# Multi-head graph attention on one core: scores' row left in PSUM, layer 3's score stage ahead of the values' linear, two memsets ahead of a subtraction

## The reference

```python
def gat_conv(x, src, dst, W, a_src, a_dst, b):
    h = (x @ W).reshape(N, H, C)
    as_n = (h * a_src).sum(-1)
    ad_n = (h * a_dst).sum(-1)
    e = jax.nn.leaky_relu(as_n[src] + ad_n[dst], NEG_SLOPE)
    m = jax.ops.segment_max(e, dst, num_segments=N)
    p = jnp.exp(e - m[dst])
    s = jax.ops.segment_sum(p, dst, num_segments=N)
    alpha = p / (s[dst] + 1e-16)
    out = jax.ops.segment_sum(alpha[:, :, None] * h[src], dst, num_segments=N)
    return out.reshape(N, H * C) + b
```

## Time and profile before

| what | value |
|---|---|
| time, median of 3 runs | 2859.42 us (2855.84 to 2861.07) |
| the profiled execution's own time | 2858.89 us |
| its span in the trace | 2856.7 us |
| busy: PE | 2709.0 us, 95% |
| busy: DVE | 1397.8 us, 49% |
| busy: ACT | 1142.1 us, 40% |
| busy: POOL | 710.3 us, 25% |
| mean granted PE clock | 0.983 |

### The profile page before, as it was taken

The page is one execution under the profiler, slowest core; times in us unless marked ns, Lnnn a source line. Parts: engine busy times, 40 slices in busy tenths (PEclk is TensorE's granted clock), DMA queues, the critical chain, the costliest instruction groups (busy, mean ns, idle before and its releaser), DMA issues. The chain is left out here.

```text
span 2856.7 us, 49216 instructions
## 1 busy us (share of the span) xinstructions
PE 2709.0 (95%) x20011; PEld 2466.1 (86%) x20011; DVE 1397.8 (49%) x3595; ACT 1142.1 (40%) x2131; POOL 710.3 (25%) x265
## 2 busy tenths in 40 slices
PE   9999999998688999998899999999998999999999
PEld 9999999995338978998897999999668897797799
DVE  9877475664122134558742552241664454302743
ACT  7633265561004203328631263332563432355431
POOL 0144311110002422220324343323204441114022
PEclk9999999999799999999999999999999999999999
DMA  2022231026992211221021222222001121111112
GB/s 67 14 76 81 86 98 40 29 84 234 413 383 74 63 39 46 67 83 41 12 89 39 67 68 78 78 67 78 29 1 46 61 71 41 60 34 35 34 45 72
DMA packets 169681, 223.22 MB, mean 78 GB/s; under 512 B 22051, under 2 KB 150719, under 8 KB 169208
## 3 DMA queue, kind: packets, MB, share of 16 engines
q1 hardware_dynamic: 169458, 220.07, 23.2%
HBM read 216.56 MB, written 3.48 MB: 77 GB/s over the span
## 5 line engine op out<-in xcount | busy, mean ns | idle before, releaser
L284 POOL TENSOR_TENSOR weights_r<-weights,head_weights_r 128x1536 fp32r<-128x1536 f32 (+1 forms) x78 | 278.7, 3573 | 1085.5 <-ACT head_weights_r L277 1075.6
L58 PE MATMUL ps<-weights_r,buf_r 128*125 128x256 f32 (+2 forms) x3794 | 510.6, 285 | 5.2 <-DVE kv L2989 1.7
L284 POOL TENSOR_TENSOR weights_r<-weights,weights_r 128x1536 fp32r<-128x1536 f32 (+1 forms) x74 | 262.4, 3546 | 907.7 <-ACT weights_r L277 907.7
L58 PEld LDWEIGHTS ps<-weights_r,buf_r 128*125 128x125 f32 x3794 | 478.0, 187 | 8.4 <-issue 3.5
L58 PE MATMUL ps<-head_weights_r,buf_r 128*125 128x256 f32 (+3 forms) x2548 | 350.7, 284 | 0.0
L58 PE MATMUL ps<-xT_r,weights_r 128*128 128x376 f32 (+3 forms) x2016 | 330.3, 309 | 0.0
L58 PEld LDWEIGHTS ps<-head_weights_r,buf_r 128*125 128x125 f32 (+1 forms) x2548 | 325.1, 187 | 0.0
L58 PEld LDWEIGHTS ps<-xT_r,weights_r 128*128 128x128 f32 x2016 | 304.7, 191 | 0.0
L58 PE MATMUL ps<-weights_r,xT_r 128*125 128x256 f32 x1680 | 231.5, 282 | 1.7 <-DVE resid L2400 0.9
L277 ACT ACTIVATE head_weights_r<-weights 128x1536 fp32r<-128x1536 f32 (+1 forms) x78 | 115.9, 1486 | 268.9 <-PE ps L58 158.1
L58 PEld LDWEIGHTS ps<-weights_r,xT_r 128*125 128x125 f32 x1680 | 211.9, 186 | 3.2 <-PE ps L2331 1.5
(11 more groups left out here) (420 smaller groups left out, 4339.8 us busy)
## 6 DMA issues: line engine op xcount, KB each, us to landing
expert_regions<-in_L_ffn_w SPq DMA_DIRECT2D x64, 576.0 KB, 12.7
expert_regions<-in_L_ffn_w SPq DMA_DIRECT2D x36, 768.0 KB, 20.4
weights<-in_L_mix_fc_w SPq DMA_DIRECT2D x24, 768.0 KB, 4.4
weights<-in_L_gnn_W SPq DMA_DIRECT2D x18, 768.0 KB, 4.5
expert_regions<-in_L_ffn_w SPq DMA_DIRECT2D x24, 384.0 KB, 9.5
weights<-in_L_ffn_W SPq DMA_DIRECT2D x11, 768.0 KB, 4.8
weights<-in_L_mix_w_mapT SPq DMA_DIRECT2D x9, 768.0 KB, 4.7
weights<-in_L_gnn_W_out SPq DMA_DIRECT2D x9, 768.0 KB, 4.5
```

Source lines behind the costliest of these rows:

```text
L58: mm = net.nc.tensor.matmul(ps, net.r(stationary(s, k)), net.r(moving(m, k)), start=(n == 0 and k == 0), stop=(stop and n == 2 and k == kc ...
L284: self.nc.gpsimd.tensor_tensor(self.r(load.dst), load.dst, self.r(load.high), ALU.subtract).then_inc(self.low_made, 1)
```

## The change

It has three parts.

1. In the `rest` stage of attentions the turns and applies are dealt over banks 0 to 5 (`ROWS` = 6), and the rows have banks 6 and 7 to themselves. For heads 1 and up the five preludes read the row from these two banks, as one access of 125x625 across both (`direct`), and the row copies are gone: 2 ACT instructions for each of 16 heads (3 x 3 in layer 0, 7 in layer 2). Rows of head n stand on PE ahead of head k's turns, where before they stood behind them and those of head 1 in the `first` stage.
2. In layer 3 the `first` stage of the attention is made ahead of the values' linear, which is now one stage of two units; before, it stood between its two units.
3. The two `Clear`s of layer 2 are made ahead of `shared`.

```diff
@@ GatHeads.step
-        ahead = n + 1 < len(self.heads)
         if k < 0 and self.begun is None:
             pe += [("row", n, j) for j in range(2)]
             act += [("row", n, j) for j in range(2)]
+        if apply and scores:
+            pe += [("row", n, j) for j in range(2)]
         if apply:
             turns = [("turn", k, s, j) for j in range(2) for s in range(NT)]
...
-        if scores and ahead:
-            pe += [("row", n + 1, j) for j in range(2)]
...
                     act.append(("leaky", n, t + 1))
-                elif ahead:
-                    act += [("row", n + 1, j) for j in range(2)]
                 act.append(("exp", n, t))
@@ GatHeads, new
+    def banks(self):
+        net = self.net
+        if not any(q[0] == "apply" for q in self.order["pe"]):
+            return super().banks()
+        ring = [net.bank() for _ in range(BANKS)]
+        held = {b % BANKS: net.freed[b - BANKS] for b in ring}
+        bank, self.prior, turn = {}, {}, 0
+        for q in self.order["pe"]:
+            if q[0] == "row":
+                b = self.ROWS + q[2]
+            else:
+                b, turn = turn % self.ROWS, turn + 1
+            bank[q], self.prior[q] = b, held[b]
+            engine, entry = self.reader(q)
+            held[b] = ({"act": net.act, "dve": net.dve}[engine].sem, self.at[engine][entry])
+        self.held = [(b, held[b % BANKS]) for b in ring]
+        return bank
+
+    def direct(self, k):
+        w = (HALVES[0][1] - HALVES[0][0]) * TP
+        return self.net.ps[:TP, self.ROWS:self.ROWS + 2, :].rearrange("p b c -> p (b c)")[:, 512 - w:512 - w + N]
@@ GatHeads.scalar
                 if t == 0:
-                    self.wait(act, "act", "row", k, 1)
+                    self.wait(act, *(("pe", "row", k, 1) if k > 0 else ("act", "row", k, 1)))
...
-                ins = nc.scalar.activation(self.P[k % 2][:, t], self.net.asb[:TP, :], ACT.Prelu, bias=self.heads[k][1][:, t:t + 1], scale=-SLOPE, alpha=1.0 / SLOPE)
+                ins = nc.scalar.activation(self.P[k % 2][:, t], self.direct(k) if k > 0 else self.net.asb[:TP, :], ACT.Prelu, bias=self.heads[k][1][:, t:t + 1], scale=-SLOPE, alpha=1.0 / SLOPE)
@@ network, layer 2's feed-forward part
-    shared = LinearT(net, pair(G[0], G[1]), [(load, 96 * k, 96, ...
     Clear(net, logits, -1.0e38)
     biases = [G[3][:64, o:o + D] for o in (D, 2 * D)]
     clear = Clear(net, biases[1])
+    shared = LinearT(net, pair(G[0], G[1]), [(load, 96 * k, 96, ...
@@ network, layer 3
     bias2 = AddRow(net, R, net.row(ins["L3_gnn_b2"]), start)
-    projected = now()
+    rest = gat_heads(net, [(tok(G[0]), 1)], D, coef, G[2], G[3], 0.0, [tok(G[4])], ins["L3_gnn_b1"], coefs=loops.ends())
     v = heads65(G[1])
-    linear_heads(net, XT, w, (2 * D, 2 * D + UNIT), by_head(v)[:, :, 0:4], evac="a", after=start)
-    rest = gat_heads(net, [(tok(G[0]), 1)], D, coef, G[2], G[3], 0.0, [tok(G[4])], ins["L3_gnn_b1"], coefs=loops.ends(), after=projected)
-    linear_heads(net, XT, w, (2 * D + UNIT, 2 * D + 2 * UNIT), by_head(v)[:, :, 4:8], evac="a", after=start)
+    linear_heads(net, XT, w, (2 * D, 2 * D + 2 * UNIT), by_head(v)[:, :, 0:8], evac="a", after=start)
     rest()
```

More of the change, by code:

```diff
@@ L2189 @@
 class Heads(Stage):
+    prior = None
     def schedule(self, n_heads, first, prior):
@@ L2207, in schedule @@
         self.bank = self.banks()
-        for q, b in self.bank.items():
+        for q, b in self.bank.items() if not self.prior else ():
             engine, entry = self.reader(q)
@@ L2242 @@
 class GatHeads(Heads):
+    ROWS = BANKS - 2
+    held = ()
     def __init__(self, net, heads, P, PT, eps, rows=(), after=None, first=-1, prior=None, begun=None):
@@ L2259, in __init__ @@
             self.at[e].update(begun.at[e])
+        for b, mark in self.held:
+            net.freed[b] = mark
         if first >= 0:
@@ L2303, in step, with wait_bank @@
         dve += outs
+    def banks(self):
[15 more added lines that the diff above has]
+        return bank
+    def wait_bank(self, pe, q):
+        if self.prior:
+            pe.wait_ge(*self.prior[q])
+        else:
+            super().wait_bank(pe, q)
+    def direct(self, k):
+        w = (HALVES[0][1] - HALVES[0][0]) * TP
+        return self.net.ps[:TP, self.ROWS:self.ROWS + 2, :].rearrange("p b c -> p (b c)")[:, 512 - w:512 - w + N]
     def reader(self, q):
-        return {"row": ("act", q), "turn": (self.turn_engine(*q[2:]) if q[0] == "turn" else "", q), "apply": ("dve", ("out",) + q[1:])}[q[0]]
+        return {"row": ("act", ("leaky", q[1], NT - 1) if q[1] > 0 else q), "turn": (self.turn_engine(*q[2:]) if q[0] == "turn" else "", q), "apply": ("dve", ("out",) + q[1:])}[q[0]]
     def tensor(self, pe):
@@ L2315, in tensor @@
                 t0, t1 = HALVES[q[2]]
-                ps = self.ps(q, TP, (t1 - t0) * TP)
+                ps = self.direct(k)[:, t0 * TP:t1 * TP] if k > 0 else self.ps(q, TP, (t1 - t0) * TP)
                 for t in range(t0, t1):
@@ L2342, in scalar @@
                 self.wait(act, "pe", *q)
-                if k > 0 and q[2] == 0:
-                    self.wait(act, "act", "leaky", k - 1, NT - 1)
                 ins = nc.scalar.activation(self.net.asb[:TP, t0 * TP:t1 * TP], self.ps(q, TP, (t1 - t0) * TP), ACT.Identity)
@@ L4226, in network @@
     hT = small(G[2], 2, 96)
-    shared = LinearT(net, pair(G[0], G[1]), [(load, 96 * k, 96, hT.chunk(k), col["mlp_b1_c"][:, k:k + 1], "gelu") for k in range(2)], "a", tiles=turned.made)
     Clear(net, logits, -1.0e38)
@@ L4230, in network @@
     clear = Clear(net, biases[1])
+    shared = LinearT(net, pair(G[0], G[1]), [(load, 96 * k, 96, hT.chunk(k), col["mlp_b1_c"][:, k:k + 1], "gelu") for k in range(2)], "a", tiles=turned.made)
     landing = [net.into(biases[1][p:p + 4, :], ins["L2_ffn_exp_b2"], clear.ends()) for p in (0, 32)]
```

## The result

The changed kernel takes 2861.70 us (median of 20 runs, 2858.78 to 2865.37), the kernel before 2858.59 us on the same chip (20 runs, 2854.12 to 2861.99). The ratio is 1.0013, 95% interval 1.0007 to 1.0019: 3.7 us slower (2.0 to 5.4), within the 0.2% that were called no change, but on the slow side, where the forecast put it. The profiled execution has a span of 2860.1 us, 3.4 more than before.

A forecast was written before the change was run, and what follows sets the result against it. PE, busy 2709.0 of 2856.7 us, was taken as the bound, so only its pauses or clock could give gains. 2.9 + 2.9 - 1.1 - 2.5 = +2.2 gave 2861.5 us; the 8-in-10 range was 2855 to 2867.

The forecast's parts named there:

- The bank wait of part 1: Attentions of several heads: turns of half 1 wait for out t = 4; +2.9 us in the 8 heads, +2.9 in layer 0.
- the 0.43 us of the sum: 8-head attention: the ten turns start 0.15 us behind out t = 4, last 1.09 us and end 0.43 us later.
- the wait for count 2: 8-head attention: PE's 0.71 us pause ahead of half 0, from which the moved rows' 1.09 us were to come out.
- PSUM preludes: Heads 1 and up: preludes reading PSUM save 0.02 us each, judged from a neighbouring exponential; bounds 0 and some 0.1.
- Part 2: Layer 3's first attention: earlier rows bring the applies near 2369.3 instead of 2370.40, -1.1 us; bounds -2.8 and +2.8.
- Alternation with POOL: Layer 3: DVE's scores and POOL's five additions alternate, one DVE operation after each POOL operation of 1.8 us.
- the ninth tile's stall: Layer 3's values' linear: v's ninth tile waits 1.2 us for the first copy, made after exponential 4 ends at 2360.7.
- the start of the applies: Layer 3's first attention: applies near 2369.3 in place of 2370.40, after the last turns wait for the fourth copy.
- Part 3: Layer 2's feed-forward part: L409 starts 1.7 us earlier, PE's pause shrinks to 1.4, clock stays up; -2.5, from -1 to -3.3.
- The slow rival: Layer 3: POOL wins twice, exponential 4 ends at 2364.6 or later, v's ninth tile stalls 5 us; 2865.4 to 2869, chance 0.17.
- The fast rival: Attentions' heads: the ring's wait hides inside PE's existing pause, heads give 0 to -1.6; 2853 to 2856 us, chance 0.16.
- the rival of no effect: Whole kernel: ACT's copies stood in a gap and all moved work is covered; 2858 to 2860 us, chance 0.15.

The follow-up runs named there:

- e4_ring_only: Kernel before with only its banks dealt as in the changed kernel (turns and applies 0 to 5, rows 6 and 7): 2864.86 against 2856.70 us, ratio 1.0032.
- e5_bank_order: Changed kernel with turns of half 1 taking the banks of half 0's turns of the same tile: 2854.40 us against 2856.73 for the kernel before, ratio 0.9993.
- e10_out_first: Changed kernel with out t = 4 ahead of sum and rinv on DVE: 2856.83 us against 2857.46 for the kernel before, ratio 0.9998.
- e8_parts_2_3: Kernel before with layer 3's reordering and the earlier memsets, without the heads' change: 2854.68 against 2856.73 us, ratio 0.9988.
- e3_memsets_only: Kernel before with only the two Clears made ahead of shared: 2856.97 against 2856.70 us, ratio 1.0004.
- e1_heads_only: Kernel before with only the heads' change (six-bank ring, rows read from PSUM, row copies gone): 2865.98 against 2856.70 us, ratio 1.0028.
- e2_layer3_only: Kernel before with only layer 3's first attention stage made ahead of the values' linear: 2857.82 against 2856.70 us, ratio 1.0004.

## Why the prediction came out as it did

**The bank wait of part 1 was right, in place, mechanism and size.** Period 11.85 for a forecast of about 11.85, 8 heads +2.8 for +2.9, layer 0's second and third attention +0.9 each as written. The first one's +0.8 for +1.1 says little, since the same code varied by 1.3 us there. e4_ring_only, e5_bank_order and e10_out_first leave nothing else for the cause. Within the 0.43 us of the sum two terms were off and cancelled: PE started 0.06 us behind out t = 4 and not 0.15, and the ten turns took 1.19 us to the applies (1350.84 to 1352.03) and not 1.09. One step was wrong without an effect: the rows do not come out of the wait for count 2, they have a wait of their own for ACT's last prelude (0.81 us). PSUM preludes at 776 ns, 804 - 776 = 28 ns less, gave about what the neighbouring row said (22). The Trainium skill's difference of fixed parts (VectorE: DVE Perf Modes, The TRN2 errata), 43 ns, lies above that.

**One cost of the ring was missing from the sum**: in layer 3 the 25 turns of an attention of one head go through six banks at a slower pace, from the first turn to the first apply 3.19 us in place of 2.80, in both attentions. The prediction had six banks in its working of the first attention ("with six banks in the ring the last turns wait for the fourth copy"), but no term for the second, +0.4. The slower pace doesn't belong to every attention of one head: in layer 2's it is 2.80 us in both kernels (1502.97 to 1505.77 before, 1509.24 to 1512.04 after).

**Part 2 was right in its steps, and its value is smaller than the sum says.** Alternation with POOL, last exponential at 18.7 us behind the sum for a forecast of 2360.7 - 2341.5 = 19.2, the ninth tile's stall (0.28 us for 1.2) and the start of the applies (27.29 us behind the sum, forecast 2369.3 - 2341.5 = 27.8, before 28.91) all fit. But most of the difference to the profile of before is that the turns had run at a low clock there; the forecast took the 4.60 us for what the kernel before always does. At equal clock the move gives 0.4 us (e8_parts_2_3 against e3_memsets_only), and in the changed kernel the ring takes that back: the applies start 27.29 us behind the sum, and 27.31 in e3_memsets_only, which has neither.

**Part 3 was mis-sized**: -2.5 us in the sum, -0.2 in the changed kernel, -0.8 in e3_memsets_only and +0.3 in e8_parts_2_3. The step that failed is "L409's input was ready long before, so after it can start near 2195.6: 1.7 earlier". The 0.54 us ahead of L409 are not a leftover of the memset; the same 0.54 stand behind L518, so only the memsets' own time, 0.8 us, was there to gain. With it fell the next step: PE's pause is 2.23 us and not 1.4. That a shorter pause keeps the clock, on which 0.8 us of the 2.5 rested, is not borne out either: behind 2.23 us it was low in the changed kernel and high in e3_memsets_only. What makes up the 0.54 us stays open.

**The sum held partly because errors cancelled.** Part 3 gave 2.3 us less than forecast, the turns of layer 3's second attention cost 0.4 more, 0.9 us lie outside the stretches, and a clock that happened to stay up gave 1.6 back. The forecast of +2.2 met +3.4 in the trace and +3.7 in the runs (2.0 to 5.4). That 2861.5 us came so near to the 2861.70 measured is luck on top: the kernel before took 2858.59 us in 20 runs, 0.8 less than in the 3 from which the forecast counted. The slow rival, an exponential 4 too late, did not occur: it ended 18.7 us behind the sum, and the rival's point, 2362, was 20.5 behind it. The fast rival, a hidden wait, is refuted by the row of 1350.84, and the rival of no effect by e1_heads_only and e4_ring_only.

## What to carry to other kernels

A ring of buffers is part of the schedule: giving two of eight banks a duty of their own moved a wait from the third to the first group of a half, and cost more than the removed copies could return, because these copies had stood in a gap. For each bank ask which reader frees it last and what stands ahead of that reader on its engine; here one rule, giving the late bank to a later user, took back some 5.7 us (ratio 0.9993 against 1.0013). Other work moved into the room that the removed copies left on ACT was worth 4 more in the 8-head attention (87.99 to 83.76 us); whether it would have fitted beside the copies was not run. Before a few microseconds in one trace are ascribed to an edit, look whether the same code ran at the same granted clock in both.

## What the runs showed of the hardware

- PE's clock behind a pause is not a function of the pause's length in these traces: behind the same 1.85 us it stayed at 1.00 in the changed kernel and fell to 0.73 over six microseconds in e2_layer3_only; behind 2.23 us it was 0.51 in the changed kernel, and in e3_memsets_only the same six transposes took 0.83 us in place of 1.48; behind 3.55 and 3.58 us, 25 transposes of the same code took 4.60 us before (clock 0.62) and 2.96 in e3_memsets_only (1.00).
- A DVE operation with two SBUF inputs and POOL's additions take turns strictly: 2.44 us for each of five scores, and the five additions 11.89 us instead of 9.02. The Trainium skill (SBUF — State Buffer, SBUF: two separate sides) describes such an exclusive lock, and this trace agrees.
- The first L409 of layer 2's feed-forward part follows its predecessor on DVE after 0.54 us, whichever that is: a memset before, L518 after. The cause is open. It is not so at the start of every stage of the kernel: before, the two memsets, each a stage, came 0.24 and 0.38 us behind their predecessors.
